# Edge network of a graph kernel: order of the heads on ScalarE, TensorE and VectorE

## What is computed

```
for h in range(4):
    K_v, V_v = x @ Kv2v[h], x @ Vv2v[h]
    K_E, V_E = edge_feature @ Ke2v[h], edge_feature @ Ve2v[h]
    alpha = concat([K_v[dst] * K_v[src], K_v[dst] * K_E]) * scale      # 128 numbers for an edge
    gate  = sigmoid(ln(alpha, ln_g[h], ln_b[h]))
    m     = (concat([V_v[src], V_E]) @ Wu[h] + bu[h]) * gate
    m     = leaky(ln(m @ Wm[h] + bm[h], mln_g[h], mln_b[h]))
    heads.append(segment_sum(m, dst))
out = concat(heads) @ Wc + bc
```

## Time and profile before

| | |
|---|---|
| three executions | 13517.1, 13525.72, 13535.36 us |
| the profiled execution | 13558.85 us, span 13556.9 us |
| busy over the span | TensorE 72%, VectorE 63%, ScalarE 50%, GpSimd 46% |
| mean granted clock of TensorE | 0.957 |
| HBM | read 1758.01 MB, written 492.97 MB |
| edge sweep of this layer | from about 4180 us to 11600 us of the span |
| chain that ended last, by engine | TensorE 45%, ScalarE 16%, GpSimd 12%, issue 10%, DMA 9%, VectorE 3% |

### The profile page before, as it was taken

The page is one execution under the profiler, slowest core; times in us unless marked ns, Lnnn a source line. Parts: engine busy times, 40 slices in busy tenths (PEclk is TensorE's granted clock), DMA queues, the critical chain, the costliest instruction groups (busy, mean ns, idle before and its releaser), DMA issues.

```text
span 13556.9 us, 195332 instructions
## 1 busy us (share of the span) xinstructions
PE 9787.2 (72%) x48422; PEld 6246.7 (46%) x48423; DVE 8520.6 (63%) x19173; ACT 6767.7 (50%) x13488; POOL 6239.9 (46%) x4199
## 2 busy tenths in 40 slices
PE   1344444444467888888888888888888888669997
PEld 0233333333225555555555555555555555323322
DVE  3233333333117787877778787877777887327896
ACT  0111111111005777777777777777777777206442
POOL 1688888888403444444444444444444444100000
PEclk9999999999997999999999999999999999889997
DMA  9766666666774444444444444444444444479763
GB/s 413 226 157 150 151 151 151 149 151 151 225 310 151 129 130 129 129 127 126 127 128 130 127 129 128 129 128 126 130 128 127 131 130 127 183 307 337 244 217 127
DMA packets 1446101, 2253.41 MB, mean 166 GB/s; under 512 B 352561, under 2 KB 981762, under 8 KB 1432131
## 3 DMA queue, kind: packets, MB, share of 16 engines
q1 hardware_dynamic: 1129144, 1975.67, 44.3%
q0 software_dynamic: 312672, 272.36, 10.9%
q10 hardware_dynamic: 4144, 3.51, 0.1%
HBM read 1758.01 MB, written 492.97 MB: 166 GB/s over the span
## 4 chain that ended last, share of the span: by engine, by line
PE 45%; ACT 16%; POOL 12%; issue 10%; DMA 9%; DVE 3%; SPq 3%; ACTq 1%; DVEq 0%; POOLq 0%; PEldq 0%
PE psum L1253 12%; POOL adj L1468 12%; ACT arena L1003 9%; PE psum L1208 6%; PE psum L1242 6%; PE psum L1340 5%; DMA arena<-adj 4%; PE psum L1268 3%; DMA adj<-put_val,put_idx 3%; PE psum L1234 3%; SPq L1515 3%; PE psum L1385 2%; ACT arena L1009 2%; PE psum L1247 2%; PE psum L1260 2%
## 5 line engine op out<-in xcount | busy, mean ns | idle before, releaser
L1468 POOL DMA_INDIRECT adj<-put_val,put_idx x1616 | 2647.9, 1639 | 844.6 <-issue 478.5
L1149 PE MATMUL psum<-ke,arena 64*128 64x256 f32 x3232 | 1451.9, 640 | 1892.3 <-DMA arena<-in_edge_t 1892.3
L1003 ACT ACTIVATE arena<-arena 128x128 f32<-128x128 f32 x6464 | 2660.4, 492 | 38.6 <-issue 35.6
L1481 POOL TENSOR_TENSOR arena<-arena,mg 128x1024 f32<-128x1024 f32 x404 | 954.9, 2364 | 3430.9 <-DVE arena L799 3430.9
L1149 PEld LDWEIGHTS psum<-ke,arena 64*128 64x128 f32 x3232 | 1041.5, 330 | 2302.3 <-issue 2035.0
L722 DVE SCALAR_TENSOR_TENSOR arena<-psum,cols,arena 128x512 f32<-128x512 f32 x1616 | 1211.3, 750 | 1228.3 <-ACT arena L1009 1068.9
L972 ACT ACTIVATE arena<-psum 128x512 f32<-128x512 f32 x808 | 482.5, 597 | 2930.7 <-PE psum L1149 2706.8
L1009 ACT ACTIVATE arena<-psum,cols 128x512 f32<-128x512 f32 x1616 | 1253.6, 776 | 1270.4 <-PE psum L1234 1270.4
L1429 POOL DMA_INDIRECT arena<-table,idx_blk x1616 | 1623.9, 1005 | 455.4 <-issue 409.2
L1242 PE MATMUL psum<-arena,wvu 128*128 128x512 f32 x3232 | 1736.4, 620 | 0.3 <-DVE arena L722 0.3
L1253 PE MATMUL psum<-wm,arena 128*128 128x64 f32 x12928 | 1717.9, 289 | 0.0
(11 more groups left out here) (218 smaller groups left out, 12814.2 us busy)
## 6 DMA issues: line engine op xcount, KB each, us to landing
arena<-adj SPq DMA_DIRECT2D x192, 1568.0 KB, 12.5
arena<-adj SPq DMA_DIRECT2D x336, 896.0 KB, 4.7
kept_keys<-arena SPq DMA_DIRECT2D x404, 512.0 KB
arena<-kept_keys SPq DMA_DIRECT2D x404, 512.0 KB
arena<-table1q SPq DMA_DIRECT2D x1616, 128.0 KB
adj<-arena SPq DMA_DIRECT2D x98, 1568.0 KB
arena<-in_edge_t SPq DMA_DIRECT2D x808, 128.0 KB, 2.6
kept_hot<-arena SPq DMA_DIRECT2D x404, 256.0 KB
```

Of the source, the lines that this page charges most:

```text
L1003: A.activation(to, at_, ACT.Identity, bias=shift[z][:, n:n + 1], scale=rstd[z][:, n:n + 1]).then_inc(normed, 1)
L1149: last = M.matmul(psum[:, 2 + 2 * z + j, t * H * D:(t + 1) * H * D], edge0[z][:, 2 * j + t, :], ke[D:P, :], start=True, stop=True)
L1468: K.indirect_dma_start(out=adj, out_offset=bass.IndirectOffsetOnAxis(ap=put_idx[s][:, j:j + 1], axis=0), in_=put_val[s][:, j:j + 1], in_of ...
```

## The change

ScalarE normalises heads 0 and 1 of group i together at the end of step i (norm 1 moves from the head of step i+1), then copies the second half product. In a step it now begins with gates 0 and 1, then take_x, norm 2, the sums, norm 3. The sums are those of group i-5, one step later than before, so that the sweep has one more step on ScalarE, and the steps outside the hardware loop load their one destination number singly. TensorE does o_pair(0) ahead of expand(i+1, 0), and turn(3), m_u(3) ahead of clear_sums and sums(0). VectorE does gate_m(3) directly behind gate_m(2), ahead of product, turn_hot and L799. The number of instructions in a step stays.

```diff
@@ VectorE, sweep1
                 if now[1]:
                     gate_m(2)
+                    gate_m(3)
                 if inside or i + 1 < NG:
                     product(i + 1, k + (s + 1) // U, (s + 1) % U)
...
                     V.tensor_tensor(y[odd], o_sb[odd], root[:, Q:2 * Q].unsqueeze(2).to_broadcast([P, Q, D]),
                                     ALU.mult).then_inc(chain2, 1)
-                if now[1]:
-                    gate_m(3)
@@ group_bases
-        def group_bases(engine, g):
-            first = dst_t[0:1, bass.ds(g * G, U * G)].rearrange("p (u t) -> p u t", t=G)[:, :, 0]
+        def group_bases(engine, g, n):
+            first = dst_t[0:1, bass.ds(g * G, n * G)].rearrange("p (u t) -> p u t", t=G)[:, :, 0]
@@ ScalarE, sweep1
-                now = [inside or 0 <= i - lag < NG for lag in range(5)]
+                now = [inside or 0 <= i - lag < NG for lag in range(6)]
-                if now[4] and s == 0:
-                    held[:] = group_bases(ACTE, i - 4)
+                if inside and s == 0:
+                    held[:] = group_bases(ACTE, i - 5, U)
+                if now[5] and not inside:
+                    held[s:s + 1] = group_bases(ACTE, i - 5, 1)
+
+                def take_sums():
+
+                    act.wait_ge(sums1, 2 * (i - 4))
+                    after(act, added1, 3 * (i - 5))
+                    for half in range(2):
+                        own = acc[:, half, bass.ds(held[s], 1)]
+                        A.activation(own, psum[:, half, 0:1], ACT.Identity, bias=own).then_inc(added1, 1)
+                    A.activation(acc[:, :, 1:NW][:, :, bass.ds(held[s], G * WIN - 1)], psum[:, 0:2, 1:G * WIN],
+                                 ACT.Copy).then_inc(added1, 1)
...
                 if now[1]:
-                    norm(i - 1, (s + 3) % U, odd, 1)
                     sigmoid(0)
-                    norm(i - 1, (s + 3) % U, odd, 2)
+                    sigmoid(1)
                 if now[0]:
...
                 if now[1]:
-                    sigmoid(1)
+                    norm(i - 1, (s + 3) % U, odd, 2)
+                if now[5]:
+                    take_sums()
+                if now[1]:
                     norm(i - 1, (s + 3) % U, odd, 3)
...
                     norm(i, s, z, 0)
+                    norm(i, s, z, 1)
                 if now[2]:
                     take_o(1)
-                if now[4]:
...
-            steps(act, sweep1, NG, 8, 4, spare=U)
+            steps(act, sweep1, NG, 8, 5, spare=U)
@@ TensorE, sweep1
                     turn(0)
                     m_u(0)
-                if now[1]:
                     turn(1)
                     m_u(1)
+                if now[2]:
+                    o_pair(0)
                 if more:
                     expand(i + 1, odd, loaded, 0)
-                if now[2]:
-                    o_pair(0)
                 if now[1]:
                     turn(2)
                     m_u(2)
                 if more:
                     expand(i + 1, odd, loaded, 1)
+                if now[1]:
+                    turn(3)
+                    m_u(3)
                 if now[4]:
                     clear_sums()
                     sums(0)
-                if now[1]:
-                    turn(3)
-                    m_u(3)
                 if now[2]:
                     o_pair(1)
```

More of the change, by code:

```diff
@@ L1044, in sweep1 @@
                     norm(i, s, z, 0)
+                    norm(i, s, z, 1)
                 if now[2]:
                     take_o(1)
-                if now[4]:
[L1048 to L1055, removed]
+            held = [None] * U
             for j in range(2):
                 take_q(0, j)
-            steps(act, sweep1, NG, 8, 4, spare=U)
+            steps(act, sweep1, NG, 8, 5, spare=U)
             for i in range(NBLK):
```

## The result

The changed kernel takes 12404.33 us (median of four executions, 12400.36 to 12406.39) against 13526.97 for the kernel before in the same comparison: a ratio of 0.917, 95% interval 0.9154 to 0.9186. It is 1123 us faster; the spans of the profiled executions differ by 13556.9 - 12402.1 = 1155 us. Here and there an execution, of the kernel before too, took over 10% longer than the others of the same kernel; the ratios leave these out.

What follows compares the result with a forecast made beforehand. No engine was full; a loop of waits between ScalarE and TensorE set 18.38 us a group. New loop 15.6 plus 0.15 for loads and clock gives 15.75, saving 1060 us over 403 groups: 12470 us, range 12300 to 12950.

Steps and rivals of the forecast that it cites:

- The loop ScalarE - TensorE, 15.6: Edge sweep: waits between ScalarE and TensorE, copy-out to copy-out, set the pace; 17.52 us a group falls to 15.6.
- The unknown wake-up: ScalarE's gate 1 might start 0.5 us late after TensorE's turn, making the loop 16.1; kept only for the range.
- 0.15 us for register loads and clock: Allowance per group, added to the 15.6 loop, for what remains of ScalarE's register loads and TensorE's low clock.
- VectorE tied with the loop: VectorE's own 15.0 us plus 0.6 waiting for GpSimd at L742 gives 15.6 at most, equal to the other loop.
- C: Rival: VectorE becomes the bound, extra wait before gate 3 or L742; period 16.7 to 17.2, 12850 to 13050 us; chance 0.14.
- Gate 3's new wait: VectorE, doing gate 3 directly behind gate 2, waits there for ScalarE's gate 3, 0.1 to 0.7 us.
- E: Rival: gate 3 holds VectorE waiting for ScalarE, slower; 19.6 us a group at 4 us, 14010 us; chance 0.05.
- TensorE's 8.3 us: Time after the copy-out at which TensorE itself reaches expand(i+1, 1), ahead of ScalarE's release at 9.3; stop of 1.0 us.
- The clock: TensorE's low-clock stretches after both stops cost 0.74 us a group; most of that was taken as gone.
- B: Rival: the 0.74 us clock loss stays; 16.46 us a group, 12750 us, or 12950 with late wake-up; chance 0.18.
- D: Rival: nothing gained, an unseen loop, a transfer or GpSimd, holds the period; time stays at 13520 us; chance 0.04.

## Why the prediction was right, and where it was not

- **The loop ScalarE - TensorE, 15.6.** Measured 15.53, and stage by stage as worked out (forecasts in brackets): gate 1 at 3.13 (3.1), the copy of q through at 9.14 (9.1), expand(i+1, 1) at 9.20 (9.3), the stop ahead of it 0.78 (1.0), from there 6.33 (6.23). The last two stages are 0.1 off each, in opposite directions. Distances between starts, taken from the old order, carried over to the new one because each engine's work stayed the same.
- **The unknown wake-up** did not come: gate 1 starts 0.04 us behind the end of turn(1). Why gate 2 of the kernel before sometimes started 0.5 us late stays open.
- **0.15 us for register loads and clock** was the term mis-sized: nothing was left of either (the steps are 15.52 to 15.56, and there is no low stretch in the sweep). The price of the loads before was right: in the runs where they stand in front of the loop's work they cost 0.50 us in one step of four (18.01 - 17.51), 0.12 a group. So the 2.86 us gained are 2.00 of loop, 0.12 of loads and 0.74 of clock. With 15.52 in the sum, 2.86 x 403 gives 1153 instead of 1060, and 13526 - 1153 = 12373; the medians moved by 30 us less than the profiled executions did.
- **VectorE tied with the loop.** Its wait at L742 came (0.34, forecast 0.6), but with that wait gone the step stayed 15.52, so C was not at work in the changed kernel. The working added up wrongly here: 1.30 + 2.36 + 2.34 + 0.1 is 6.10 and not 6.2, and 1.13 + 2 x 1.6 + 2 x 0.67 is 5.67 and not 5.6, so that the wait comes to 0.43 us and VectorE's period to 15.4, just under the other loop and not tied with it. The run with the sums late fits this: with 1.2 us taken out of the first loop, the step fell only to 15.41.
- **Gate 3's new wait** is next to nothing: the two gates take 1.53 us together at 8014.73 and 0.75 us each, which leaves 0.03 us between them (forecast 0.1 to 0.7). E was rightly small; but the part does nothing either, nor does turn(3), as each put back showed.
- **What the working left out** is what o_pair(0) ahead of expand does by itself. It stands there only inside TensorE's 8.3 us. Alone it is worth 1.46 us of loop and the clock's 0.74, more than any other part but ScalarE's, which contains the same gain. The two are not a sum: 6.3% and 8.3% alone, 8.3% together.
- **The clock.** That the 0.74 us goes was right, the reason given only in part: both stops around turn(1) were named, and the second alone decides. That the low stretch shown came right behind both stops spoke for nothing, since every step has both. B is refuted by the granted clock of 1.00. The Trainium skill, "TensorE: Matmul & The Clock Gate" (What's actually happening), says that the low clock is the default and that activity releases it. The run in which 404 useless products save 266 us (13506.18 - 13240.38) agrees; the run in which as many, one place earlier, save nothing shows that the rule does not tell where the activity has to be.
- **D** is refuted: TensorE kept all its instructions and the kernel is 8.3% faster. The Trainium skill, "Perfetto Trace Analysis" (Identifying the Most-Contended Engine), says to optimise the engine with the highest occupancy first. It does not say, as D takes it, that the time stays where that engine keeps its work, and the trace agrees with the page in so far as the gain lay in TensorE's stops, 2.6 us a group before and 0.8 after. What the busy shares of 85, 79 and 76% could not show is which wait to shorten.

## What to carry to other kernels

When no engine is full, follow one period from a hand-over back to itself and look at what stands in front of each wait in the other engine's list: a piece of ready work moved into the gap (o_pair ahead of expand) can be worth most of what shortening the path that causes it gives (6.3% and 8.3% here), and doing both gives the gain once. Take the parts of a change both out of the new kernel and alone into the old one. "Can be removed without loss" and "is worth nothing" are different statements. Look at the granted clock by step when TensorE stops: a stop costs its length and may cost the clock, and which stop it is has to be tried.

## What was not expected of the hardware

Of the two stops of a step the shorter one, 1.26 us behind m_u(1), preceded all 96 low stretches of the kernel before, and none is left once 0.86 us of it are filled; the 1.38 us behind m_u(0) could be filled without effect, and could stay without harm (1.49 in the mean of the run with m_u(1) twice, clock 1.00). In another order stops of 0.46 to 1.47 us behind clear_sums came before 60 low stretches, and with gate 3 last in that order six still followed stops of only 0.47 to 0.56 us in the same place, while the changed kernel stops for 0.78 us ahead of expand in every group and has no low stretch in its sweep. Most stops have no consequence: in the kernel before there are 96 low stretches to some 400 groups with both stops. So the length of the idle time does not by itself tell which stop costs the clock in this kernel; what does was not tried further.
